# Filler products on TensorE in the last steps of a mixture-of-experts pass (language-model tower, one core)

## The reference, cut to what matters

```python
logits = x @ gate_w + gate_b                      # 8 experts
topk_vals, topk_idx = top_k(logits, 2)
weights = softmax(topk_vals) at the chosen experts
h = relu(x @ w1 + b1)                             # per expert, 128 -> 256
expert_out = h @ w2 + b2                          # 256 -> 128
out = x_before + sum over experts of expert_out * weights
```

## Time and profile before

| | |
|---|---|
| median of 3 runs | 2561.26 us |
| the profiled execution, its time | 2562.14 us |
| its span, first to last instruction | 2560.4 us |
| TensorE matmul busy | 2283.6 us (89%) |
| DVE, ScalarE, GpSimd busy | 74%, 66%, 58% |
| mean granted clock of TensorE | 0.97 |
| DMA, mean over the span | 140 GB/s |

### The profile page before, as it was taken

One profiled execution on the slowest core, in us unless ns is written; L12 is line 12 of the kernel. 1 busy time (PEld: TensorE's weight loads), 2 busy tenths in 40 slices (PEclk: granted clock), 3 DMA queues, 4 the chain that ended last, 5 costly groups with the idle time before them and its releaser, 6 DMA issues.

```text
span 2560.4 us, 60070 instructions
## 1 busy us (share of the span) xinstructions
PE 2283.6 (89%) x16943; PEld 1992.8 (78%) x16943; DVE 1883.7 (74%) x8436; ACT 1687.9 (66%) x5272; POOL 1483.0 (58%) x1870
## 2 busy tenths in 40 slices
PE   4999978688886999999999999999999999999854
PEld 4777756455553888888888899999999888999854
DVE  4777756666663788888888887887788888888622
ACT  3777744122222877777777778888887777788643
POOL 6444200377775678888888864444444666467553
PEclk9999989899998999999999999999999999999977
DMA  2575630244445411111111156566556777487687
GB/s 74 197 242 201 237 123 1 69 152 147 147 149 163 102 40 47 43 48 43 47 43 48 43 144 167 161 165 172 164 139 190 215 217 203 120 243 208 178 255 238
DMA packets 343689, 357.45 MB, mean 140 GB/s; under 512 B 36491, under 2 KB 285931, under 8 KB 343360
## 3 DMA queue, kind: packets, MB, share of 16 engines
q1 hardware_dynamic: 305856, 265.69, 36.6%
q0 software_dynamic: 34048, 80.03, 9.5%
q10 hardware_dynamic: 3456, 7.89, 1.0%
HBM read 211.02 MB, written 136.67 MB: 136 GB/s over the span
## 4 chain that ended last, share of the span: by engine, by line
PE 54%; DVE 20%; issue 7%; DMA 7%; POOL 7%; ACT 3%; SPq 2%; DVEq 0%; ACTq 0%; POOLq 0%
PE bank L2081 6%; PE bank L2171 6%; PE bank L2157 5%; PE bank L2092 4%; PE bank L2124 4%; PE bank L2132 4%; PE bank L2080 3%; PE bank L2104 3%; PE bank L2106 3%; PE bank L2105 3%; DVE pr_place L1584 2%; PE bank L2037 2%; DMA rows<-table,idx 2%; PE bank L2050 2%; DVE nmax L1564 2%
## 5 line engine op out<-in xcount | busy, mean ns | idle before, releaser
L881 POOL DMA_INDIRECT zbuf<-pc,kb x248 | 250.7, 1011 | 240.7 <-DVE pc L1749 189.8
L866 POOL DMA_INDIRECT spread_rows<-kb,pos x256 | 256.9, 1004 | 152.0 <-DVE pc L1749 69.8
L1088 ACT ACTIVATE pr_place<-bank,nmax 128x128 f32<-128x128 f32 x512 | 188.2, 368 | 214.1 <-DVE nmax L1564 213.8
L2081 PE MATMUL bank<-xT,gT 128*128 128x256 f32 x1024 | 306.5, 381 | 0.0
L1584 DVE COPY pr_place<-bank 128x384 f32<-128x384 f32 x512 | 281.2, 549 | 9.1 <-PE bank L2092 7.7
L2171 PE MATMUL bank<-wvo_part,x_part 128*128 128x512 f32 x768 | 268.9, 458 | 0.0
L1563 DVE TENSOR_REDUCE nmax<-bank 128x1 f32<-128x128 f32 x512 | 143.3, 280 | 170.2 <-PE bank L2081 168.0
L2092 PE MATMUL bank<-ident,pr_place 128*128 128x128 f32 x1536 | 253.0, 274 | 16.1 <-DVE pr_place L1584 15.8
L1098 ACT ACTIVATE bank<-causal 128x384 f32<-128x384 f32 x512 | 253.4, 495 | 19.5 <-PE bank L2215 3.3
L2092 PEld LDWEIGHTS bank<-ident,pr_place 128*128 128x128 f32 x1536 | 196.4, 141 | 84.8 <-DVE pr_place L1577 19.9
L2157 PE MATMUL bank<-x_part,wqk_part 128*128 128x256 f32 x1536 | 245.8, 296 | 1.2 <-DVE x_part L1691 1.2
(11 more groups left out here) (340 smaller groups left out, 6517.4 us busy)
## 6 DMA issues: line engine op xcount, KB each, us to landing
pa<-bundle SPq DMA_DIRECT2D x198, 321.0 KB
table<-rows SPq DMA_DIRECT2D x96, 576.0 KB
rows<-table SPq DMA_DIRECT2D x192, 128.0 KB
wu_more<-bundle SPq DMA_DIRECT2D x66, 321.0 KB
junk<-zbuf SPq DMA_DIRECT2D x32, 512.0 KB, 5.0
kb<-spread_rows SPq DMA_DIRECT2D x248, 65.0 KB
h3buf<-h SPq DMA_DIRECT2D x64, 128.0 KB, 1.9
kb<-kb SPq DMA_DIRECT2D x32, 256.0 KB
```

What stands on the lines that cost most here:

```text
L866: pool.indirect_dma_start(out=spread_rows, out_offset=bass.IndirectOffsetOnAxis(ap=pos[:, k, j:j + 1], axis=0), in_=xr4s[g % 2][:, k, j], ...
L2081: pe.matmul(s2[:, P:3 * P], g[:, P:2 * P], xT3[:, p], start=False, stop=True, skip_group_check=True)\
```

## The change

Behind attention, from the first step whose slot is at least U + 2 x H1 = 528 (step 260, x = 254), TensorE issues fillers into bank 3 ahead of three of its waits: two ahead of the wait for unit x's rows and weights, one ahead of the wait for hTu, two ahead of the wait for xTu. A part that is missing in a step has no fillers either.

```diff
         INSIDE = min(c for u, c in STEP_AT.items() if u >= U + H1)
+        TAIL = min(c for u, c in STEP_AT.items() if u >= U + 2 * H1)
         SLOT_OF = {STEPS[c][0]: u for u, c in STEP_AT.items() if STEPS[c][0] is not None}
...
                 if x is not None:
+                    if c >= TAIL:
+                        stay_warm(SBANK[0], 2)
                     if x < RING:
                         pe.wait_ge(xu_in[x % WR], 32 * (x // WR + 1))
                     else:
                         pe.wait_ge(end_in[(x - RING) % ER], end_there(x - RING))
                     ins = pe.transpose(xy_bank(c)[:, 0:P], xu_at(x)[:, 0:C], ident[:])
                 if down is not None:
+                    if c >= TAIL:
+                        stay_warm(SBANK[0], 1)
                     pe.wait_ge(hTu_ready, down + 1)
                     for k in range(2):
                         ins = pe.matmul(xy_bank(c)[:, P:2 * P], hTu[:, down % 3, k], wu_at(down)[:, F1 + k * C:F1 + (k + 1) * C],
                                         start=(k == 0), stop=(k == 1))
                 ins.then_inc(xy_mm, 1)
                 if up is not None:
+                    if c >= TAIL:
+                        stay_warm(SBANK[0], 2)
                     pe.wait_ge(xTu_ready, up + 1)
```

## The result

Over 20 runs of each the change takes 2569.60 us (median, 2561.81 to 2575.27) and the kernel before 2563.49 (2557.01 to 2568.10). The ratio is 1.0021, 95% interval 1.0012 to 1.0031: slower by 5.4 us (3 to 8), under the 0.3% that the prediction took as its bound for "no change". The forecast was 5.0 us on 2561.26 us, so 2566.3 with a range of 2561 to 2570.5; the measured 2569.60 lies inside it, 3.3 us above, of which 2.2 us are the kernel before itself, whose median over 20 runs is that much higher.

What follows compares the result with a forecast made beforehand. In the last 120 us SyncE's queue delivering units, not TensorE on average, was taken as the bound. TensorE ends 8 us later, 3 hidden by DVE's wait: 5.0 on the median 2561.26 gives 2566.3 us, range 2561 to 2570.5.

Steps and rivals of the forecast that it cites:

- The price of a filler: A float16 product of 512 columns on TensorE: 0.215 us at full clock, so a step with all five takes 2.08 us.
- Stretches 1 and 2: Steps 260 to 274 and 275 to 283: gaps of 8.42 and 4.87 us behind them absorb the fillers, cost 0.
- Stretch 3: Steps 284 to 307: 108 fillers of 23.2 us leave TensorE no gap; its last product ends 8 us later.
- What reaches the end: Last results and scatters: DVE's wait of 3.04 us hides 3 of the 8 us, leaving 5.0 us.
- The feedback: Row loads waiting for scatters twelve units back: SyncE waits some tenths, later perhaps 1 to 2 us; cost 0.
- rival C: The loop of loads closes as low clock holds TensorE at step 284: end 9 us later, 2570.3 us; chance 0.20.
- Rival B: Fillers behind step 284 are hidden, that stretch ending 4 to 5 us below the sum: 2562 us; chance 0.27.
- Rival D: Faster by over 7.7 us, which would need earlier data from SyncE's queue; chance 0.03.

Runs made afterwards that it cites:

- e1: Changed kernel with twice as many fillers at each of the three places (4, 2, 4; 430 in all): 2592.64 us against 2560.50, ratio 1.0123.
- e3: Changed kernel with fillers in the first 24 steps only (260 to 283): 2558.84 us, ratio 0.9991 to the kernel before.
- e4: Changed kernel with fillers in the last 24 steps only (from 284 on): 2565.55 us, ratio 1.0023 to the kernel before.
- e8: Changed kernel with seven fillers a step (3, 1, 3): ratio 1.0007 (0.9977 to 1.0038) to the kernel before, which took 2824.90 us in that set.
- e9: The kernel before, unchanged, run for a profile on another chip: ratio 1.0007 (0.9975 to 1.0040), with the kernel before at 2820.62 us.
- e11: Kernel before plus fillers only ahead of the wait for rows in eleven steps with gaps, second run, on another chip: ratio 0.9996 (0.9961 to 1.0032).
- e10: Changed kernel with seven fillers a step (3, 1, 3), second run, on another chip: ratio 1.0014 (0.9980 to 1.0048) to the kernel before.

## Why the prediction was right

**The price of a filler** was right: 0.215 us in another stage, the same here (2.07 us for a step, forecast 2.08). The Trainium skill (TensorE: Matmul & The Clock Gate, section Back-to-back issue gap) gives about 131 ns for such a product in a sustained stream. The traces disagree for this stream: 0.215 us in the step above, and e1's 135.8 us need 0.215 a filler. By 131 ns a full step would be 1.67 us, as an estimate, under the supply of 1.89.

**Stretches 1 and 2 cost nothing**: shown by e3 (0.5 us more to 5 us less than before). The 2.17 us gap at step 262 closed as forecast and the clock stayed up there (1.00 for 2440 to 2460). Of the 8.42 and 4.87 us gaps 6.80 and 3.28 were left; I had forecast 2.5 for the second. The low clock behind it came as forecast too: 2496.06 to about 2501.9, 5.8 us against the 4.9 that I took.

**Stretch 3**: forecast 8.0 us later from step 284 on, measured 8.3 (48.9 against 40.6), all of it without a gap; shown by e4, and its law (work plus 0.2155 a filler) by e8 and e1. Counted from step 284, step 290 starts 3.4 us later than before and step 301 5.3, forecast about 3 and 5.

**What reaches the end** was the term that was off in size. The step reads: "its wait of 3.04 us hides 3 of the 8. I take 5.0." From step 284's transpose to the end of the span it is 67.9 us against 61.4, 6.5 more, so 1.7 were hidden, not 3. DVE's last wait did shrink, to 0.42 us, and the last scatter landed 0.95 us sooner after its start. But it started 3.56 us after DVE began its last result (2545.70 and 2549.26), where the prediction took the 1.17 of before: GpSimd stood idle for 2.28 us ahead of scatter 293 (2546.45), though DVE had made its input by 2543.75, and scatters 294 and 295 follow it one behind the other. The chain names nothing for it ("issue"). The same 2.28 us are in e4 at the same scatter, and only 1.06 stood there before. It isn't the fillers alone: the unchanged kernel has 2.56 us there in e9. SyncE's loads of result group 29 had gone out some 2 to 4 us ahead of that idle time in after and e4, but before the change too, so they don't tell the cases apart; its cause is open. Over the 20 runs the difference is 5.4 us by the ratio and 6.1 by the medians, between the forecast 5.0 and the profile's 6.5. The interval, 3 to 8 us, can't tell these apart, so that the time falls so near 5.0 is in part luck.

**The feedback** did not close: the waits of L679 are 3.5 us. Even where it does close (e1, 20.6 us of waits), it costs nothing while TensorE is the slower. That was argued and is now shown, and it rules out rival C in this form. Rival B, in which stretch 3 ends 4 to 5 us below the sum, is ruled out by D, 48.9 with the change and 48.7 in e4. Rival D, faster by over 7.7 us, did not come with the change, and no run shows it. The smaller gain that a higher clock could bring without the cost of the fillers is another matter, and is not settled.

What stays open is a possible gain of a few us by fillers in the gaps or in the first 24 steps alone (0.9991 with 0.9980 to 1.0002 for the latter). No version was shown to beat the kernel before.

## What to carry to other kernels

Before an idle-looking engine is given work to keep its clock, compare the step with that work to the supply of data, not the busy share: here 1.01 us had room up to 1.89. Five a step (2.08 us) cost 5 us; two (1.44) left L as it was, and their time was measured too coarsely to say more. Count only the fillers that fall into a gap as hidden; in an engine that executes in order those of a burst are delay. A raised clock is not yet a gain: the change took the granted clock from 0.82 to 0.98 in the 40 us behind 2500 and made the kernel slower. And take both ends of a distance with care: the same 8.1 us from the last load to the last product came about in two different ways in e9 and e11.

## What the runs showed of the hardware beyond that

- Narrow float16 fillers (128 columns, 0.055 us each) lengthened the float32 products beside them from 0.45 to 0.50 us for four; wide ones did not (0.445).
- At step 284 a start at the low clock came behind gaps of 3.28 us (after), 3.07 (e10) and 5.17 (e4). It lasted 5.8 us in after (to about 2501.9), 5.5 in e4 (to about 2499.8) and 2.8 in e10 (2747.33 to about 2750.1), although in all three the steps were packed with fillers; in the kernel before it lasted 4.9. So more work behind the gap did not end it sooner as a rule.
- The same kernel took 2560 us in one set and 2820 to 2825 in the next two, with 35 runs each in these. One of them was on the same chip as the set ahead. A 0.2% effect could not be read there in the times. Distances between two landmarks of a profile showed it in part, but the stage itself was 15 us longer in the unchanged kernel, so such distances hold only against a profile of the same set.
